# State-space slots: the output projection in plain fp32, and the scaling for the state moved to GpSimd

## The reference, cut to what matters

```
proj = xn @ in_proj_w.T;   z, xc, B, C, dt = split(proj)
xc   = silu(conv_b + sum over 4 taps of conv_w * shifted xc)
h_t  = exp(A*dt_t) * h_(t-1) + B_t (outer) x_t          # x_t = xc at token t, by heads
y_t  = h_t . C_t + D_param * x_t
y    = rms(y) * inner_norm_w * silu(z)
out  = y @ out_proj_w.T;   result = x + out
```

## Time and profile before

| | us |
|---|---|
| median of 3 runs | 3035.02 (3034.8 to 3040.43) |
| span of the profiled execution | 3067.1 |
| PE busy (share of the span) | 2711.5 (88%) |
| PEld busy | 2120.1 (69%) |
| DVE busy | 2384.6 (78%) |
| ACT busy | 2110.9 (69%) |
| POOL busy | 1973.4 (64%) |

### The profile page before, as it was taken

The page is one execution under the profiler, slowest core; times in us unless marked ns, Lnnn a source line. Parts: engine busy times, 40 slices in busy tenths (PEclk is TensorE's granted clock), DMA queues, the critical chain, the costliest instruction groups (busy, mean ns, idle before and its releaser), DMA issues.

```text
span 3067.1 us, 58582 instructions
## 1 busy us (share of the span) xinstructions
PE 2711.5 (88%) x17318; PEld 2120.1 (69%) x17318; DVE 2384.6 (78%) x5972; ACT 2110.9 (69%) x4670; POOL 1973.4 (64%) x1697
## 2 busy tenths in 40 slices
PE   4799999998569888379799999999999999999997
PEld 2466666665469765267588788787887878878786
DVE  3466666666377589558599999998899999999896
ACT  4444454443255466346599999998999999999996
POOL 3322222214424214555399999998999999999998
PEclk7799999997889899689899999999999999999999
DMA  6355445455766544446777776767666666676673
GB/s 168 94 176 170 168 165 185 149 195 168 238 178 199 168 154 151 157 128 199 230 240 237 236 237 205 220 204 220 219 206 217 205 210 216 205 224 199 203 218 113
DMA packets 320436, 588.35 MB, mean 192 GB/s; under 512 B 47888, under 2 KB 138800, under 8 KB 319632
## 3 DMA queue, kind: packets, MB, share of 16 engines
q1 hardware_dynamic: 305776, 545.07, 57.6%
q0 software_dynamic: 14352, 39.54, 3.5%
HBM read 464.44 MB, written 124.17 MB: 192 GB/s over the span
## 4 chain that ended last, share of the span: by engine, by line
POOL 34%; issue 10%; ACT 3%; DVE 1%; PE 1%; DMA 1%; POOLq 1%; SPq 0%; ACTq 0%; DVEq 0%
POOL mm L2706 8%; POOL y L2719 7%; POOL yz L2723 7%; POOL y L2733 6%; POOL y_lo L2712 6%; ACT mt L2636 1%; DVE cv L2789 1%; DMA wi<-ssm_wi_split 1%; POOLq L2382 1%; ACT ys L2650 0%; ACT mt L2656 0%; DVE bank L2860 0%; ACT L2671 0%; POOL first L2748 0%; PE bank L64 0%
## 5 line engine op out<-in xcount | busy, mean ns | idle before, releaser
L2706 POOL TENSOR_TENSOR mm<-mt,cb 128x512 f32<-128x512 f32 x384 | 490.2, 1299 | 56.9 <-ACT mt L2656 54.9
L2636 ACT ACTIVATE mt<-a_wide,a_tok 128x128 f32<-128x128 f32 x1536 | 487.1, 389 | 3.5 <-POOL mm L2706 2.5
L2789 DVE SCALAR_TENSOR_TENSOR cv<-bank,taps,cv 128x509 f32<-128x509 f32 (+2 forms) x576 | 429.3, 745 | 13.6
L64 PE MATMUL bank<-f,wi 128*128 128x512 f32 x768 | 322.4, 420 | 14.7 <-DMA wi<-ssm_wi_split 14.6
L65 PE MATMUL bank<-f,wi 128*128 128x512 f32 x768 | 305.7, 398 | 0.0
L66 PE MATMUL bank<-f,wi 128*128 128x512 f32 x768 | 305.7, 398 | 0.0
L2723 POOL TENSOR_TENSOR yz<-y,zs 128x512 f32<-128x512 f32 x192 | 249.2, 1298 | 15.0
L2712 POOL TENSOR_TENSOR y_lo<-yz,y_hi 128x512 fp32r<-128x512 f32 x192 | 246.2, 1282 | 8.4 <-ACT y_hi L2661 6.5
L2719 POOL TENSOR_TENSOR y<-t 128x512 f32<-128x512 f32 x192 | 246.0, 1281 | 0.0
L2529 PE MATMUL bank<-mm,x_tok 128*64 128x128 f32 x3072 | 226.4, 283 | 13.1 <-POOL mm L2706 13.1
L2733 POOL TENSOR_TENSOR y<-y,ys 128x512 f32<-128x512 f32 x184 | 237.6, 1292 | 0.1
(11 more groups left out here) (476 smaller groups left out, 8067.5 us busy)
## 6 DMA issues: line engine op xcount, KB each, us to landing
wi<-ssm_wi_split SPq DMA_DIRECT2D x192, 512.0 KB
a_wide<-a_scratch SPq DMA_DIRECT2D x192, 512.0 KB
l_fw<-ffn_split SPq DMA_DIRECT2D x72, 768.0 KB
ea<-ea_scratch SPq DMA_DIRECT2D x384, 128.0 KB
wo<-ssm_wo_split SPq DMA_DIRECT2D x192, 256.0 KB, 4.1
sorted_scratch<-ex_zeros SPq DMA_DIRECT2D x96, 130.5 KB
ssm_wi_split<-l_s_out SPq DMA_DIRECT2D x24, 512.0 KB
ey_x<-sorted_scratch SPq DMA_DIRECT2D x94, 130.5 KB
```

The lines of the kernel that those rows point to most:

```text
L64: pe.matmul(out, wh, xh, start=first, stop=False)
L2636: i = act.activation(mt[:, h, chunk(j)], a_wide[:, g % R, h, chunk(j)], ACT.Relu, bias=a_tok[:, s * NJ + j, 2 * t + h:2 * t + h + 1], scal ...
L2706: pl.tensor_tensor(mm[:, :, ts], mt[:, :, ts], cb[:, js, :].rearrange("p j t -> p (j t)") .unsqueeze(1).broadcast_to([P, 2, TS // 2]), ALU ...
L2789: dve.scalar_tensor_tensor(cv[:, a:TS], bank[:, X, 0:TS - a], taps[:, t, k:k + 1], cv[:, a:TS], ALU.mult, ALU.add).then_inc(ph["tap"], 1)
```

## The change

`project_out` multiplies yz itself by plain fp32 weights: two fp32 matmuls in place of six fp32r ones, after yz instead of y_lo. y_hi (ACT) and y_lo (POOL) are gone. wo holds 256 columns instead of 512, and so does its copy in DRAM. `to_end` goes from DVE to POOL, behind `decayed`, in the place of y_lo; it reads x_tok in SBUF instead of bank XT. The waits on xd that guarded XT (in turn, mean_square and tanh) go; `tokens` now waits for xd of the slot before, as xd reads x_tok; yz waits for out instead of y_lo. In the weight split ACT copies the 512 input columns first, then waits for DVE's scaling and copies the 256 output columns unrounded; POOL subtracts 512 columns for these tiles.

```diff
                 def high(n):
...
                     split_in(act, n)
                     split_kept(act, n - 1)
-                    if n >= NT:
-                        done(act, "s_wo", n - NT)
-                    act.activation(s_out[:, 0:MLP], s_raw[:, 0:MLP], ACT.Copy).then_inc(ph["high"], 1)
+                    if n < NT:
+                        act.activation(s_out[:, 0:MLP], s_raw[:, 0:MLP], ACT.Copy).then_inc(ph["high"], 1)
+                        return
+                    act.activation(s_out[:, 0:MP_IN], s_raw[:, 0:MP_IN], ACT.Copy)
+                    done(act, "s_wo", n - NT)
+                    act.activation(s_out[:, MP_IN:MLP].bitcast(F32), s_raw[:, MP_IN:MLP], ACT.Copy).then_inc(ph["high"], 1)
...
-                    pl.tensor_tensor(s_out[:, MLP:2 * MLP], s_raw[:, 0:MLP], s_out[:, 0:MLP].bitcast(F32), ALU.subtract).then_inc(ph["low"], 1)
+                    w = MLP if n < NT else MP_IN
+                    pl.tensor_tensor(s_out[:, MLP:MLP + w], s_raw[:, 0:w], s_out[:, 0:w].bitcast(F32), ALU.subtract).then_inc(ph["low"], 1)
...
-        wo = sb("wo", [P, R, 2 * MP_OUT], F32R)
+        wo = sb("wo", [P, R, MP_OUT])
...
                 def project_out(g):
                     t, s = g % NCT, g // NCT
-                    done(pe, "y_lo", g)
+                    done(pe, "yz", g)
                     landed(pe, "wo", g)
...
                     for m in range(KD):
-                        a = m * P
-                        i = mm3(pe, bank[:, OUT + m, :], (wo[:, g % R, a:a + P], wo[:, g % R, MP_OUT + a:MP_OUT + a + P]),
-                                (y_hi[:], y_lo[:]), t == 0, t == LAST)
+                        i = pe.matmul(bank[:, OUT + m, :], wo[:, g % R, m * P:(m + 1) * P], yz[:, g % 2], start=t == 0, stop=t == LAST)
                     i.then_inc(ph["out"], 1)
...
                 def turn(g):
                     done(pe, "xs", g)
                     done(pe, "x_tok", g - 1)
-                    done(pe, "xd", g - 1)
...
                 def tanh(g):
                     done(act, "tap", g, NR)
                     done(act, "x_tok", g - 1)
-                    done(act, "xd", g - 1)
...
-                def output_high(g):
-                    done(act, "yz", g)
-                    done(act, "out", g - 1)
-                    act.activation(y_hi[:], yz[:, g % 2], ACT.Copy).then_inc(ph["y_hi"], 1)
-
                 def tokens(g):
                     done(act, "xt", g)
                     done(act, "intra", g - 1)
+                    done(act, "xd", g - 1)
...
-                def output_low(g):
-                    done(pl, "y_hi", g)
-                    done(pl, "out", g - 1)
-                    pl.tensor_tensor(y_lo[:], yz[:, g % 2], y_hi[:].bitcast(F32), ALU.subtract).then_inc(ph["y_lo"], 1)
+                def to_end(g):
+                    s, t = g // NCT, g % NCT
+                    done(pl, "x_tok", g)
+                    done(pl, "u", g - 1)
+                    pl.tensor_tensor(xd[:].rearrange("p j (h c) -> p j h c", h=2), x_tok[:].rearrange("p j (h c) -> p j h c", h=2),
+                                     w_tok[:, s * NJ:(s + 1) * NJ, 2 * t:2 * t + 2].unsqueeze(3)
+                                     .broadcast_to([P, NJ, 2, PH]), ALU.mult).then_inc(ph["xd"], 1)
...
-                    done(pl, "y_lo", g - 2)
+                    done(pl, "out", g - 2)
                     pl.tensor_tensor(yz[:, g % 2], y[:], zs[:, g % NS], ALU.mult).then_inc(ph["yz"], 1)
...
                 for k in BEATS:
                     if has(k - 1):
                         decayed(k - 1)
-                    if has(k - 4):
-                        output_low(k - 4)
+                        to_end(k - 1)
```

More of the change, by code:

```diff
@@ L129, in program @@
         wi_dram = nc.dram_tensor("ssm_wi_split", (NCT, P, 2 * MP_IN), F32, kind="Internal").ap()
-        wo_dram = nc.dram_tensor("ssm_wo_split", (NCT, P, 2 * MP_OUT), F32, kind="Internal").ap()
+        wo_dram = nc.dram_tensor("ssm_wo_scaled", (NCT, P, MP_OUT), F32, kind="Internal").ap()
         a_drams = (a_dram, nc.dram_tensor("a_scratch1", (HM, T), F32, kind="Internal").ap())
@@ L428, in keep @@
                     else:
-                        parts = s_out[:].bitcast(F32).rearrange("p (h c) -> p h c", h=2)
-                        sp.dma_start(wi_dram[n - NT].rearrange("p (h c) -> p h c", h=2), parts[:, :, 0:MP_IN]).then_inc(ph["s_kept"], 16)
-                        sp.dma_start(wo_dram[n - NT].rearrange("p (h c) -> p h c", h=2), parts[:, :, MP_IN:MLP]).then_inc(ph["s_kept"], 16)
+                        parts = s_out[:].bitcast(F32)
+                        sp.dma_start(wi_dram[n - NT].rearrange("p (h c) -> p h c", h=2),
+                                     parts.rearrange("p (h c) -> p h c", h=2)[:, :, 0:MP_IN]).then_inc(ph["s_kept"], 16)
+                        sp.dma_start(wo_dram[n - NT], parts[:, MP_IN:MLP]).then_inc(ph["s_kept"], 16)
                 def clear(a):
@@ L2365, in ssm @@
         yz = sb("yz", [P, 2, TS])
-        y_hi, y_lo = sb("y_hi", [P, TS], F32R), sb("y_lo", [P, TS], F32R)
         y2, yr = sb("y2", [P, TS]), sb("yr", [P, TS])
@@ L2430, in weights_out @@
                     done(sp, "out", g - R)
-                    sp.dma_start(wo[:, g % R, :].bitcast(F32), wo_dram[g % NCT]).then_inc(ph[f"wo{g % R}"], 16)
+                    sp.dma_start(wo[:, g % R, :], wo_dram[g % NCT]).then_inc(ph[f"wo{g % R}"], 16)
                 def inputs(s):
@@ L2571, in mean_square @@
                     done(pe, "x_tok", min(s * NCT + LAST + 3, N - 1))
-                    done(pe, "xd", min(s * NCT + LAST + 3, N - 1))
                     done(pe, "xs", min(s * NCT + LAST + 4, N - 1))
@@ L2680, in _ @@
                         convolve(k)
-                    if has(k - 4):
-                        output_high(k - 4)
                     if has(k):
@@ L2845, in state_part @@
                     dve.tensor_tensor(t1[:], bank[:, INTER, :], ea[:, g % R], ALU.mult).then_inc(ph["t1"], 1)
[L2847 to L2854, removed]
                 def evacuate(s):
@@ L2869, in _ @@
                         evacuate(e // NCT)
-                    if has(k - 1):
-                        to_end(k - 1)
                     if has(k):
```

## The result

The changed kernel takes 3056.86 us (median of 4 runs, 3052.02 to 3058.55) where the kernel before took 3036.20 (4 runs on the same chip, 3034.80 to 3040.43): 20.7 us more, a ratio of 1.0063 with a 95% interval of 1.0048 to 1.0077. So it is slower, as forecast, by half of the 42 us of the sum. The time lies 0.1 us under the lower end of the range.

What follows compares the result with a forecast made beforehand. The prediction took PE and POOL to tie in the slots (beats of 7.65 and 7.67 us), with the longer projection making PE's 7.98. Its terms summed to +42 on the median of 3035: 3077 us, range 3057 to 3104.

Steps and rivals of the forecast that it cites:

- the sum: All terms over slots, step ends, tail and first stage together: +42 us, added to the median of 3035.
- the tie: In the slot stage PE's free beat is 7.65 us and POOL's 7.67; the longer projection makes PE's 7.98.
- The terms of 84, 33 and 20 beats: Slot beats going to 7.98 us: 84 from 7.67 (+26), 33 with edges from 7.82 (+5), 20 from 8.08 (-2).
- Expert rows: Thirty slot beats where PE also turns expert rows go from 7.86 to 8.19 us: +10 us.
- Rival 1: POOL alone bounds the slots and PE has room, so not slower: 3030 us, or 2994 with xd at 1.09; 10%.
- Rival 2: xd is on PE's path in the slots, update waits 0.48 us: +88, 3165 us, or 3121 with half; 15%.
- the first stage: In the weight split ACT copies 512 columns ahead of its wait for DVE: gain 0 to 12 us, taken as 2.
- late xd: In the slots PE's update waits for xd from POOL, 0 to 0.05 us a beat, 0 to 9 us; taken as +4.
- ends of seven steps: Pairs of beats at step ends: first -0.4 us, second +0.6 for xd and +0.33 for the projection; +3.5 in all.
- tail: In the drain POOL's chain loses two y_lo ahead of a y, 1.28 us each: -2.5 us.
- low case of 3061: Lower end of the forecast: projection grown by 0.32 us, no late xd, all 12 us of the first stage.
- the smaller projection: On PE the projection grows by 0.32 us, the low end of 0.32 to 0.44; 0.33 was taken.

Runs made afterwards that it cites:

- plain_alone: The kernel before with only the projection changed to two plain fp32 matmuls, y_hi and y_lo still made but unread; 3069.77 us, 1.0120 of the kernel before.
- xd_on_dve: The changed kernel with xd back on DVE, read from bank XT; 3054.86 us, 1.0068 of the kernel before.
- one_pass: The changed kernel with the projection as two fp32r matmuls, low products left out, less exact; 2970.12 us, 0.9785 of the kernel before.
- y_on_dve: The kernel before with ACT's new order in the weight split, xd moved to POOL and y's addition to DVE; 3023.74 us, 0.9963 of the kernel before.

## Why the prediction was right in its direction and wrong in its size

**Right: the tie, and what breaks it.** Steady beats of 7.95 (forecast 7.98), project_out at 1.72 (1.72 to 1.84), POOL with gaps of 0.36 to 0.41 ended by ACT (0.3 to 0.5), a square without a wait, no wait named on PE. The terms of 84, 33 and 20 beats made 26 + 5 - 2 = +29; ordinary and edge beats together measured 17.9 + 9.6 = +27.5. Expert rows: +10 forecast, +10.2 measured. plain_alone shows the cause in isolation, +36 us for the two matmuls alone.

**Rival 1 is out.** POOL's beat did fall, to 7.41, and PE had no room. The Trainium skill's rule for judging TensorE by its weight-load share (Perfetto Trace Analysis, Identifying the Most-Contended Engine) would have given this rival; here 0.3 us more on PE showed in full, with weight loads busy 49.26 us of 60 and 45.21 after. The starts of the matmuls, without a gap, were the better reading. **Rival 2 is out** as well: xd is 0.24 early, and xd_on_dve leaves the beat at 7.95.

**The step that failed is the first stage.** The prediction bounded the gain of ACT's new order by "some 0.5 us in each, 12 us, and at least nothing" and took 2, with no row that spoke for the low end. POOL's shorter subtraction in the same split had no term at all. Measured: 14.3 us with both edits of the split, 12.0 for the order alone, 9.0 for it in the kernel before. The bound itself was a little short as well, as the 512 columns take 0.62 us, 15 us in 24 places, not 0.5. That ACT waits 73.5 us in 24 places did not say what a shorter wait is worth. A likely reading, not shown, is that ACT's queue runs in order and other work stands behind that wait; which of that work carries the gain to the end of the stage was not taken apart.

**Smaller terms.**

| term | forecast | measured |
|---|---|---|
| late xd | +4 | 0: xd takes 1.055 us, not 1.28 |
| ends of seven steps | +3.5 | +2.1 (-0.43 and +0.73 a pair, forecast -0.4 and +0.93) |
| tail | -2.5 | -3.0 to -4.3 |
| beats 78 and 79 | none | -4.4 |

For the late xd the prediction had a range of 1.09 to 1.30 for the operation, by which xd ends at 3.89 to 4.10, not at its 3.85 to 4.06. The low end, l_qb, was the nearer row, with an operand spread in the same way; by it xd ends at 3.89, ahead of the 3.99 when it is due, and the term is 0. The gain in beats 78 and 79 was in no row that the prediction read: PE waits there for the input weights, which come behind the load of the second sequence's states. These two beats take 17.0 to 17.8 us in the kernels with xd on POOL and beats of 7.95 or more, 18.5 and 19.3 in one_pass and y_on_dve, which have xd on POOL and shorter beats, and 21.0 to 23.3 in those with xd on DVE. Why they are shorter stays open.

From the forecast's +42 the first stage takes 12, the late xd 4, beats 78 and 79 another 4, and the tail, the ends of steps and the ordinary beats some 4 together. That would make +18; the timed runs say +20.7. The 3 us between are of the size by which single executions differ (3052.02 to 3058.55 for after), and no run assigns them.

**The range** ended at 3057 on a low case of 3061 that had "all 12 us of the first stage", the smaller projection and no late xd. All three came about, within 0.01 us a beat. What lay below it is what the sum had not bounded: the 2 us more of the first stage, the tail, and beats 78 and 79.

## What to carry to other kernels

Where two engines tie, as here, relieving one returned next to nothing and loading the other cost in full: lay the engine's own unhindered beat beside every change to it. A wait in an in-order queue ahead of filler work is cheap to move behind the part that doesn't need it. Bound what that is worth by the length of the work that moves; here 9 and 12 us came back of 14.9, so an estimate at the low end needs a row that speaks for it. And when the best version is sought, separate the parts: here the small edit of ACT's order was the gain (0.9966), and the headline edit the loss (1.0120).

## What was not expected of the hardware

A product on POOL of a 512-element tile with a table spread along its innermost axis takes 1.055 us, where products and sums of two full tiles take 1.27 to 1.30 in the same beats. And an operation of DVE with two inputs in SBUF took 1.6 us beside POOL's work where one with an input in PSUM took 0.69, and delayed POOL's next operation by 0.43 besides.
